# Graph attention on one core: transfers of 125 rows cut into 112 and 13, an earlier normalisation, layer 2 maxima in four parts

## The reference

```python
def _gat_layer(x, src, dst, W, a_src, a_dst, bias, concat):
    h = (x @ W).reshape(N, H, C)
    al_s = einsum('nhc,hc->nh', h, a_src); al_d = einsum('nhc,hc->nh', h, a_dst)
    e = leaky_relu(al_s[src] + al_d[dst], 0.2)
    m = segment_max(e, dst); ex = exp(e - m[dst])
    denom = segment_sum(ex, dst)
    msg = h[src] * (ex / (denom[dst] + 1e-16))[:, :, None]
    return segment_sum(msg, dst) + bias
h   = elu(_gat_layer(x, src, dst, W1, as1, ad1, b1, concat=True))     # (1250, 2048)
out = _gat_layer(h, src, dst, W2, as2, ad2, b2, concat=False)         # (1250, 768)
y = layernorm(x + out)
```

## Time and profile before

| | us |
|---|---|
| median of 3 runs (lowest, highest) | 1078.98 (1078.12, 1080.71) |
| the profiled execution | 1085.29 |
| its span | 1083.5 |
| busy: PE, PEld | 884.8 (82%), 807.9 (75%) |
| busy: DVE, ACT, POOL | 638.8 (59%), 421.0 (39%), 249.0 (23%) |
| mean DMA rate, 112.60 MB moved | 104 GB/s |

### The profile page before, as it was taken

How to read it: one execution, slowest core, us unless ns; L and a number is a source line. 1 busy time by engine, 2 the same in 40 slices (tenths; PEclk the granted TensorE clock), 3 DMA queues, 4 the chain that set the end, 5 groups by cost and what they waited for, 6 DMA issues and landing times. The chain is left out here.

```text
span 1083.5 us, 14761 instructions
## 1 busy us (share of the span) xinstructions
PE 884.8 (82%) x5572; PEld 807.9 (75%) x5572; DVE 638.8 (59%) x1245; ACT 421.0 (39%) x679; POOL 249.0 (23%) x165
## 2 busy tenths in 40 slices
PE   0666558955989998999989997986999999279696
PEld 0444336545978898988978897986989998279696
DVE  9666327544786488745986488671212214487783
ACT  6344221124753376425754275751111110177300
POOL 1002000003921255203721256400000000055450
PEclk9987768986999998999999998998999999689898
DMA  5039864425235442545225333332111212110131
GB/s 148 2 96 143 139 192 143 151 86 171 91 99 182 128 140 87 187 133 176 71 84 179 100 112 112 109 129 86 57 65 41 66 56 77 41 61 2 50 108 57
DMA packets 56119, 112.60 MB, mean 104 GB/s; under 512 B 25004, under 2 KB 26414, under 8 KB 54418
## 3 DMA queue, kind: packets, MB, share of 16 engines
q1 hardware_dynamic: 54749, 108.53, 34.2%
q10 hardware_dynamic: 1300, 3.13, 1.1%
HBM read 86.71 MB, written 24.94 MB: 103 GB/s over the span
## 5 line engine op out<-in xcount | busy, mean ns | idle before, releaser
L554 POOL TENSOR_TENSOR pbuf<-pbuf,grow 125x625 f32<-125x625 f32 x100 | 166.1, 1661 | 698.5 <-ACT grow L1093 246.8
L1515 PE MATMUL ps<-hx,PThi 125*125 125x260 f32 (+5 forms) x800 | 231.5, 289 | 25.1 <-DVE vbuf L1291 15.6
L1517 PE MATMUL ps<-hx,PTlo 125*125 125x260 f32 (+5 forms) x800 | 229.3, 287 | 0.0
L1516 PE MATMUL ps<-hlo,PThi 125*125 125x260 f32 (+4 forms) x800 | 229.2, 286 | 0.0
L1515 PEld LDWEIGHTS ps<-hx,PThi 125*125 125x125 f32 x800 | 153.2, 191 | 29.2 <-issue 23.0
L1516 PEld LDWEIGHTS ps<-hlo,PThi 125*125 125x125 f32 x800 | 153.6, 192 | 1.5
L1517 PEld LDWEIGHTS ps<-hx,PTlo 125*125 125x125 f32 x800 | 153.4, 192 | 0.0
L567 DVE SCALAR_TENSOR_TENSOR pbuf<-pbuf,counts 125x625 f32<-125x625 f32 x100 | 107.7, 1077 | 58.3 <-ACT pbuf L561 58.2
L1515 PE MATMUL ps<-W2p,hT 128*125 128x384 f32 x320 | 110.4, 345 | 3.9 <-DVE hT L1303 2.7
L1516 PE MATMUL ps<-W2p,hT 128*125 128x384 f32 x320 | 108.5, 339 | 0.0
L1517 PE MATMUL ps<-W2p,hT 128*125 128x384 f32 x320 | 108.4, 339 | 0.0
(11 more groups left out here) (175 smaller groups left out, 1662.5 us busy)
## 6 DMA issues: line engine op xcount, KB each, us to landing
xr<-xT_scratch SPq DMA_DIRECT2D x30, 750.0 KB, 10.1
nbm<-mask_scratch SPq DMA_DIRECT2D x40, 305.2 KB
hidden_scratch<-vbuf SPq DMA_DIRECT2D x40, 250.0 KB
hblk<-hidden_scratch SPq DMA_DIRECT2D x10, 1000.0 KB
xT_scratch<-xa SPq DMA_DIRECT2D x20, 375.0 KB, 12.0
w1raw<-in_L_gnn_W SPq DMA_DIRECT2D x4, 1536.0 KB, 7.8
w1raw<-in_L_gnn_W SPq DMA_DIRECT2D x12, 512.0 KB, 5.3
w2raw<-in_L_gnn_W SPq DMA_DIRECT2D x14, 384.0 KB, 6.7
```

What stands on the lines that cost most here:

```text
L554: pool.tensor_tensor(pslot(c), pslot(c), src[:, g * GN:(g + 1) * GN], ALU.add).then_inc(e_done, 1)
L1515: pe.matmul(dst, ahi, bhi, start=start, stop=False, skip_group_check=shared)
L1516: pe.matmul(dst[:, 0:n], ahi, blo, start=False, stop=False, skip_group_check=shared)
L1517: return pe.matmul(dst, alo, bhi, start=False, stop=stop, skip_group_check=shared)
```

## The change

1. Every transfer between HBM and 125 partitions is issued as two, partitions 0 to 111 and 112 to 124 (`RP`), on the same semaphore, and the waits count twice as far (`RS` = 32). The loads of x at the start are so already; transfers with 128 partitions (`xT_d`, `xr`, `w1raw`, `w2raw`, `attr`) stay whole. SP issues about 170 transfers more, ACT ten.
2. `evict_group` takes the place of five `evict`: sums and reciprocals are made for blocks 0 and 1 in one instruction each, then for blocks 2 to 4. It stands in the chunk with b = 0, after its low part and the next chunk's counts, and ahead of `split_h`.
3. Layer 2's maxima cover columns 0:500, then three parts of 250. They run between VectorE's steps for blocks 5 to 9 of the W2 product; only the last part comes after. There are four buffers for the first mask part and one for each of the others; `load_hb(b + 3)` is issued ahead of the store of block b's score, and `load_hb(2)` ahead of the layer 2 masks. Each part waits for its own blocks' scores.
4. The shift row of layer 2 is spread and copied in two halves.
5. `evict2(0)` and `evict2(1)` go ahead of VectorE's last low part. The last output block is made, evicted, normalised and stored by column halves, the right one (with the sums) first on TensorE.

```diff
+RP = ((0, 112), (112, B))
+RS = 16 * len(RP)
...
-                sp.dma_start(nbm[:, i % MR, :], nb_d[b]).then_inc(ld_nb[i % MR], 16)
+                for lo, hi in RP:
+                    sp.dma_start(nbm[lo:hi, i % MR, :], nb_d[b, lo:hi, :]).then_inc(ld_nb[i % MR], 16)
...
-            sp.wait_ge(w2_lo, KC - W2F)
+            load_hb(2)
             for b in range(M2):
                 load_nb2(b)
-            for b in range(2, NB):
-                load_hb(b)
-                store_s2(b - 2)
-                load_s2(b - 2)
-            for b in range(M2, 5):
-                load_nb2(b)
-            sp.wait_ge(ht_ps, 2 * NB)
-            sp.dma_start(nbl[:], nb_d[:, :, N8:].rearrange("b p n -> p b n")).then_inc(ld_nbl, 16)
-            for b in range(5, NB):
-                load_nb2(b)
-            store_s2(NB - 2)
-            load_s2(NB - 2)
+            load_part(0)
+            for b in range(NB - 1):
+                if b + 3 < NB:
+                    load_hb(b + 3)
+                elif b + 3 == NB:
+                    sp.wait_ge(ht_ps, 2 * NB - 2)
+                    load_part(1)
+                else:
+                    sp.wait_ge(ht_ps, 2 * NB)
+                    load_part(2)
+                store_s2(b)
+                load_s2(b)
+                if b == 4:
+                    for i in range(M2, 2 * M2):
+                        load_nb2(i)
+                if b == 5:
+                    for i in range(2 * M2, NB):
+                        load_nb2(i)
...
-                act.dma_start(nb_d[b], nbs[:]).then_inc(nb_stored, 16)
+                for lo, hi in RP:
+                    act.dma_start(nb_d[b, lo:hi, :], nbs[lo:hi, :]).then_inc(nb_stored, 16)
...
+            def denominators(q, part):
+                lo, hi = ((0, 2), (2, GT))[part]
+                n = GT * q
+                dve.wait_ge(ag, ag_block(q, hi - 1))
...
+                dve.tensor_scalar(deps[:, n + lo:n + hi], sums, 1e-16, None, ALU.add).then_inc(d_eps, 1)
+                dve.wait_ge(d_eps, 2 * q + part + 1)
+                dve.reciprocal(rden[:, n + lo:n + hi], deps[:, n + lo:n + hi]).then_inc(d_done, 1)
+                dve.wait_ge(d_done, 2 * q + part + 1)
...
+            def evict_group(q):
+                denominators(q, 0)
+                evict(q, 0)
+                evict(q, 1)
+                denominators(q, 1)
+                for t in range(2, GT):
+                    evict(q, t)
+
             for c in range(CHUNKS):
                 h, g, b = chunk_of(c)
-                if b == 2 and c >= NB:
-                    for t in range(GT):
-                        evict(c // NB - 1, t)
                 dve_lo(dve, c)
                 if c + 1 < CHUNKS:
                     dve_counts(dve, c + 1)
+                if b == 0 and c >= NB:
+                    evict_group(c // NB - 1)
                 if g == 0 and b < 3 and h > 0:
                     split_h(NB * h + NB - 3 + b)
...
             for b in range(NB):
                 if b > 0 and b + 1 < NB:
                     split_hT(2 * b + 2)
...
+                if b in (5, 6):
+                    for m in range(4):
+                        maxima2(4 * (b - 5) + m)
+                if b == 7:
+                    maxima2(8)
+                    maxima2(9)
+                    for m in range(4):
+                        part_maxima2(0, m)
+                if b == 8:
+                    for m in range(4, NB):
+                        part_maxima2(0, m)
+                    merge(0)
                 if b + 1 < NB:
                     split_hT(2 * b + 3)
...
+                if b == NB - 1:
                     for m in range(NB):
-                        last_maxima2(0, m)
-                    dve.wait_ge(mx_last, NB)
-                    merge(0)
+                        part_maxima2(1, m)
+                    merge(1)
                 scores2(b)
...
             for c in range(CHUNKS, CHUNKS + 2 * NB):
+                if c == CHUNKS + 2 * NB - 1:
+                    evict2(0)
+                    evict2(1)
                 dve_lo(dve, c)
...
+                    for i in (1, 0):
+                        for b in range(NB):
+                            last = piece2(NB + b, t, i, True)
+                        last.then_inc(ag2, 1)
```

More of the change, by code:

```diff
@@ L408, in gat_kernel @@
         y_b = sem("y_b")
+        y_half = sem("y_half")
         xb_done = sem("xb_done")
@@ L671, in store_hid @@
                 sp.wait_ge(hid_done, n + 1)
-                sp.dma_start(hid_d[j * B:(j + 1) * B, h * HC:(h + 1) * HC], vbuf[:, n % GT, :]).then_inc(hid_stored[n % GT], 16)
+                for lo, hi in RP:
+                    sp.dma_start(hid_d[j * B + lo:j * B + hi, h * HC:(h + 1) * HC], vbuf[lo:hi, n % GT, :]).then_inc(hid_stored[n % GT], 16)
             def load_w2(c):
@@ L682, in load_hb @@
                     sp.wait_ge(ht_ps, 2 * b - 2)
-                sp.dma_start(hblk[:, b % 2, :], hid_d[b * B:(b + 1) * B, :]).then_inc(ld_hb[b % 2], 16)
-            sp.wait_ge(nb_stored, 16 * NB)
+                for lo, hi in RP:
+                    sp.dma_start(hblk[lo:hi, b % 2, :], hid_d[b * B + lo:b * B + hi, :]).then_inc(ld_hb[b % 2], 16)
+            sp.wait_ge(nb_stored, RS * NB)
             for b in range(MR):
@@ L1333, in _ @@
             split_hT(0)
-            for t in range(GT):
-                evict(NG - 1, t)
+            evict_group(NG - 1)
             lo_w2(8)
@@ L1381, in last_maxima2 @@
                 dve.memset(gate[:], 0.0)
-                dve.tensor_tensor_reduce(out=junk2[:, 0:B], in0=nbl[:, b, part * B:(part + 1) * B],
-                                         in1=arow2[:, N8 + part * B:N8 + (part + 1) * B], scale=1.0,
-                                         scalar=-3.0e38, op0=ALU.add, op1=ALU.max, accum_out=mx[:, i:i + 1]).then_inc(mx_last, 1)
-            def merge(part):
+                dve.tensor_tensor_reduce(out=junk2[:, 0:QW], in0=nbp[p][:, b, :], in1=arow2[:, N4 + p * QW:N4 + (p + 1) * QW], scale=1.0,
+                                         scalar=-3.0e38, op0=ALU.add, op1=ALU.max, accum_out=mxp[:, i:i + 1]).then_inc(mx_last, 1)
@@ L1387, in merge @@
+            def merge(p):
                 lo, hi = H * NB, (H + 1) * NB
-                dve.tensor_tensor(mx[:, lo:hi], mx[:, lo:hi], mx[:, lo + (1 + part) * NB:hi + (1 + part) * NB], ALU.max).then_inc(mx_all, 1)
+                dve.wait_ge(mx_last, (p + 1) * NB)
+                if p > 0:
+                    dve.wait_ge(mx_all, p)
+                dve.tensor_tensor(mx[:, lo:hi], mx[:, lo:hi], mxp[:, p * NB:(p + 1) * NB], ALU.max).then_inc(mx_all, 1)
             for b in range(NB):
@@ L1709, in _ @@
             pe.wait_ge(g_done, H + 1)
-            spread(lambda n: gcol[:, H * NB + n:H * NB + n + 1], four_from(4)).then_inc(bc2_ps, 1)
+            for g in range(2):
+                spread(lambda n: gcol[:, H * NB + n:H * NB + n + 1], lambda n: (4 + n // GT * 2 + n % GT // BB, n % GT % BB * B),
+                       g * GT, (g + 1) * GT).then_inc(bc2_ps, 1)
             pe.wait_ge(h2x_one, 1)
-            pe.wait_ge(g2_sb, 1)
+            pe.wait_ge(g2_sb, 2)
             def piece2(c, t, i, first):
```

259 lines of the change are left out of this document (147 added, 112 removed).

## The result

| | kernel before | changed kernel |
|---|---|---|
| median (lowest, highest), us | 1079.73 (1078.12, 1080.71), 4 runs | 1018.47 (1014.29, 1019.02), 4 runs |
| ratio, 95% interval | | 0.943 (0.940 to 0.945) |
| profiled execution, its span | 1085.29, 1083.5 | 1014.29, 1012.4 |

The change makes the kernel 61.3 us faster by the medians. The forecast was 1009, in a range from 989 to 1033: sign and range hold, and the time came out 9.5 above the forecast.

What follows compares the result with a forecast made beforehand. TensorE is busy nearly throughout the long stages, so only its idle stretches can give. Terms -19 -5.5 -17 -19 +13 -17 -1.6 -3.5 = -69.6 gave 1015 profiled, 1009 as median after taking over 6.3; range 989 to 1033.

Steps and rivals of the forecast that it cites:

- A1: Mask stores at the start, cut into 112 and 13 rows: ScalarE's waits shrink, 19 us gained, ends 9 and 24.
- A2: First ten maxima, 225 to 249 us: most of VectorE's idling ahead of mask blocks goes, 5.5 us gained, ends 3 and 7.5.
- A3: Loads of `hblk` in the W2 product: shorter loads and an earlier first one remove the waits, 17 us gained, ends 12 and 18.
- B, the four boundaries: Group ends with no W1 product following: five blocks normalised after the first low part, 19 us gained, ends 12 and 21.
- B, the three boundaries ahead of W1: Head to next head: low part of h stands behind the normalisation, TensorE waits about 3.8, 13 us lost, ends 6 and 19.
- plus 2.4 each: Added TensorE wait at each of three boundaries ahead of W1, 7.2 us for three, before the clock loss.
- C: Layer 2 maxima in four parts: first addition 12 us after the last W2 product, not 29.2; 17 gained, ends 12 and 19.
- A: All transfers of 125 rows as 112 and 13, on 16 engines instead of 5; its terms give 38.5 us.
- D: Output product and end: 1.6 us from two blocks normalised ahead of the last low part, 3.5 at the end.
- Rival 2: Stores of transposed x hold the start, W1 waits grow to 4.8: A1 10 less, B 6 more lost; 1025 us, chance 0.22.
- rival 1: Paired transfers go one behind the other, DMA terms give nothing: -31, 1048 us, chance 0.06.
- rival 3: Slower: each pair's second transfer adds full latency at the mask stores, up to 1105 us, chance 0.03.

Runs made afterwards that it cites:

- mixed cuts: Changed kernel with hidden-layer block loads 3 to 8 cut otherwise (whole, 120+5, 64+61, 80+45, 124+1, 96+29); 1020.2 us in one run.

## Why the prediction was right, and where it was not

**What the cut does to a transfer** was right in kind: 5 engines against 16, by the DMA share, and the mixed cuts show the rule in seven cases. Its size was put low. From issue to the last row a steady load took 13.0 to 14.0 us before (the first row 4.6 to 5.5 behind the issue, then 8.3 to 8.5) and 5.3 to 5.9 after (0.9, then 4.4 to 4.9): 8 shorter, not 5. The time ahead of the first row was not in my estimate.

**A1** (-19; 9 to 24): 12 by the mask stores left whole. The failing step is the estimate of 6 us for a cut store's landing; it is 10.6 to 11. Of the 24 us by which I expected the first chunk earlier, 21.9 came in the first pair of profiles, but only 17.5 with the cut taken out of the changed kernel (257.3 to 239.7) and 17.7 with it put into the kernel before, which is A1 and A2 (12 and 6). The other 4 belong to the paragraph on the time below. **A2** (-5.5): TensorE's wait ahead of the first spread fell from 16.80 to 10.84 and is 16.75 without the cut: 6.0, right.

**A3** (-17): the product with W2 became 19.9 shorter. The mechanism was half right. I read the waits for `hblk` as the load's own length. The load can be 12 us long at no cost when SP issues it in time; what took the time before was SP's loop of store, wait and reload, every step of which is a transfer of 125 rows. The moved first load, to which I gave 5 of the 17, gave nothing that can be seen: the cut alone reaches 187.3 in the old order, and the new order without the cut stays at 207.6.

**What no term held.** The cut also took the old waits of 1.69 to 2.01 ahead of the W1 products and the low clock behind one of them: 7.7 us at three boundaries (43.0 to 35.4). I had taken them as part of VectorE's queue and as given; they came from mask loads and the shift row's round trip.

**B, the four boundaries** (-19; 12 to 21): -14.7 to -16.3, inside the ends; TensorE's pauses for `vbuf` there are 0, 0.4, 0.7 and 1.8 us, so tenths at three of the four. **B, the three boundaries ahead of W1** (+13; 6 to 19): the pauses were 3.7 to 3.9, as forecast at 3.8. With nothing cut the loss is 13.7 (43.0 to 56.7), the forecast's value. But with the cut, whose kernel has no pause there at all, it is 18.1 to 18.7. The step that failed is "plus 2.4 each": it takes the old 1.69 off the new 3.8 as if both stood ahead of the same W1 product. They do not (b = 8 and b = 9), and without the new order the cut removes the old wait by itself. So B is a loss of 4 where I had a gain of 6, and the two edits together give less than their sum. One pair of lines exchanged gets both sides.

**C** (-17; 12 to 19): the stretch became 17.7 shorter, the first addition came 11.4 behind the last product (forecast 12), and a maximum over 250 columns recurs every 0.47 us (forecast 0.5). But the cut alone gives 7.9 of it, and the maxima without the cut 2.3 (34.5 to 32.2), since VectorE waits 13.1 us for a score row that comes back late. My sentence on the ninth block's round trip took its old 14 us to be hidden; it was hidden only once shortened. The terms were added as if independent, and this one rests on A.

**D** (-1.6 and -3.5): -1.1 and -3.9; at the end 2.8 of it are the cut's.

**The sum** came out at -69.6 and the pair of profiles at -71.0, and that they agree is in part luck. Stage by stage the forecast was near; by cause it gave too little to A (38.5 against 57) and too much to B and C, and the errors cancelled. Rival 2 had the direction of both its halves, less at the mask stores (12, not 19) and more at the W1 boundaries (18, not 13), but not its reason for the second: the pauses stayed at 3.7 to 3.9 and did not grow to 4.8. Its total of 1025 was not reached, for what was missing elsewhere made up for both. Two slips of the prediction change nothing here: by its own terms the ends add to about -90 and -33, not -89 and -34, and the gains outside the DMA terms are 31 in its rival 1 and 28 in its rival 3.

**The time.** 1009 fell 9.5 short although the sum agrees with the profiles. The step that failed is the last: the assumption that the profiled execution's distance of 6.3 to the median can be carried over. The profile of before lay 5.6 above the median of the four runs beside the result, and that of after 4.2 below its own. Executions of the kernel before differ by more than those of the changed one: medians from 1076.9 to 1087.9 in three groups, where the changed kernel took 1014 to 1020 in all nine runs that are its own or the same but for mixed cuts. In the profile of the kernel with nothing cut, whose transfers up to there are those of the kernel before, the first chunk started 3.4 us earlier (257.3, not 260.7), and TensorE's waits of the earlier trace rows were 0.5 to 0.9. I take it that the 6 us lay in the waits for transfers which the cut removes, so that they had to be taken off the gain; a second profile of the kernel before was not made, so this is argued, not shown.

## What to carry to other kernels

Before anything is rearranged around a slow transfer, read the DMA share while it runs alone: a share of 0.3, 0.26 or 0.06 is a row count that deals badly onto 16 engines, and cutting off the 13 rows that 16 does not divide was worth 57 us here, of 59 that the whole change gave in the same group; the rest of the change gave 2 without it and some 10 with it. Price an edit at a queue against the kernel as it will be, not as it was: a wait that another part of the change removes, or that stands ahead of another product, is no credit. Where two moved steps meet, put the one first whose consumer has nothing else to do (the low part: 0.7 us of work against 4.7).

## What the runs showed of the hardware that I had not expected

- SP took 16.45 us to issue four mask loads of 125 rows while earlier transfers were under way, and 4.42 for the same data in eight cut ones.
- From a store of 125 values of 4 bytes to the reload that waits for its landing it took 5.8 us (scores whole, loads cut) to 21.6 us (behind 61 rows on one engine).
- The first row of a lone cut load of 1 MB moved 0.9 us behind its issue; behind a reload of one row spread over the partitions it was 3.3 (cut) and 4.6 to 6.0 (whole).
- TensorE's pauses of 3.7 to 3.9 us ahead of a W1 product cost 1.5 to 2.8 us more behind them, with a granted clock of 0.58 and 0.71 in the two windows above.
